# A depthwise-and-projection convolution on one core: an opening that waits for half of image 0, and GpSimd sums that alternate between two tiles

## The reference

```python
v = groupnorm(x)                   # 32 groups = every channel alone, over 64 x 64
xd = concat(v[:, :, 0::2, 0::2], v[:, :, 0::2, 1::2],
            v[:, :, 1::2, 0::2], v[:, :, 1::2, 1::2])   # 128 channels, 32 x 32
feats = concat(dwconv(xd, w1, 1), dwconv(xd, w3, 3), dwconv(xd, w5, 5))
y = einsum('bchw,oc->bohw', feats, w_proj)              # 384 -> 128 channels
out = x + interleave(y)            # the four quarters of y go back to the 2 x 2 positions
```

## Time and profile before

| | |
|---|---|
| median of 3 runs | 137.13 us (136.56 to 137.18) |
| the profiled execution | 136.35 us, of which the trace spans 134.5 us |
| busy | TensorE 94%, VectorE 90%, GpSimd 87%, ScalarE 82% |
| granted TensorE clock | 0.99 on the mean |

### The profile page before, as it was taken

One profiled execution on the slowest core, in us unless ns is written; L12 is line 12 of the kernel. 1 busy time (PEld: TensorE's weight loads), 2 busy tenths in 40 slices (PEclk: granted clock), 3 DMA queues, 4 the chain that ended last, 5 costly groups with the idle time before them and its releaser, 6 DMA issues.

```text
span 134.5 us, 1577 instructions
## 1 busy us (share of the span) xinstructions
PE 126.2 (94%) x519; PEld 97.2 (72%) x519; DVE 120.6 (90%) x147; ACT 110.5 (82%) x118; POOL 117.5 (87%) x89
## 2 busy tenths in 40 slices
PE   5998999999999999999999999999999999999920
PEld 5866888888886888688886888688867688778700
DVE  6579799998799999999999999999999999999660
ACT  2589989999999999999999999999999999060000
POOL 6261999999999999999999999999999999999930
PEclk9999999999999999999999999999999999999996
DMA  3999999990044008097999879693799478989176
GB/s 71 270 258 199 204 202 203 193 189 5 2 80 80 0 0 163 3 117 110 187 124 90 166 156 112 100 188 72 78 103 185 107 78 78 117 134 202 25 169 138
DMA packets 35847, 16.67 MB, mean 124 GB/s; under 512 B 34048, under 2 KB 34176, under 8 KB 35456
## 3 DMA queue, kind: packets, MB, share of 16 engines
q0 software_dynamic: 1488, 6.93, 38.6%
q1 hardware_dynamic: 32720, 9.18, 36.2%
q10 hardware_dynamic: 1632, 0.48, 2.0%
HBM read 5.46 MB, written 4.19 MB: 72 GB/s over the span
## 4 chain that ended last, share of the span: by engine, by line
PE 88%; DMA 4%; ACT 2%; ACTq 1%; DVEq 1%; DVE 1%; issue 0%
PE YP L700 77%; PE YP L763 10%; DMA w_sb<-in_L_conv_w_dram 4%; ACT weff L401 2%; ACT HI L411 1%; DVEq L102 1%; DVE X L657 1%; ACTq L377 0%; ACTq L376 0%; PE YP L675 0%; PE YP L688 0%; ACT coef L395 0%; PE YP L682 0%; ACT coef L406 0%; ACTq L397 0%
## 5 line engine op out<-in xcount | busy, mean ns | idle before, releaser
L324 POOL TENSOR_TENSOR RING_SUM<-RING_SUM,PROD 128x900 f32<-128x900 f32 (+1 forms) x45 | 92.8, 2066 | 3.5
L621 DVE SCALAR_TENSOR_TENSOR ACC<-G,coef,ACC 128x930 f32<-128x930 f32 (+1 forms) x57 | 68.2, 1196 | 1.8
L461 ACT ACTIVATE PROD<-G,coef 128x900 f32<-128x900 f32 (+1 forms) x45 | 44.5, 1050 | 0.0
L700 PE MATMUL YP<-HI,wlo 128*128 128x512 f32 (+2 forms) x148 | 38.8, 412 | 0.0
L700 PE MATMUL YP<-HI,whi 128*128 128x512 f32 (+2 forms) x148 | 36.6, 398 | 0.7 <-ACT HI L411 0.7
L700 PE MATMUL YP<-LO,whi 128*128 128x512 f32 (+2 forms) x148 | 37.2, 401 | 0.0
L700 PEld LDWEIGHTS YP<-HI,wlo 128*128 128x128 f32 x148 | 27.9, 189 | 8.7 <-issue 2.9
L700 PEld LDWEIGHTS YP<-HI,whi 128*128 128x128 f32 x148 | 27.7, 189 | 7.8 <-ACT HI L411 1.1
L700 PEld LDWEIGHTS YP<-LO,whi 128*128 128x128 f32 x148 | 27.9, 189 | 7.1 <-issue 1.0
L421 ACT ACTIVATE G<-X,nbias,rstd 64x1024 f32<-64x1024 f32 x16 | 21.1, 1318 | 0.8 <-DVE nbias L533 0.5
L442 ACT ACTIVATE Y<-YP 64x1024 f32<-64x1024 f32 x14 | 15.3, 1095 | 4.4 <-PE YP L763 4.1
(11 more groups left out here) (67 smaller groups left out, 61.8 us busy)
## 6 DMA issues: line engine op xcount, KB each, us to landing
X<-in_x_dram SPq DMA_DIRECT2D x16, 256.0 KB, 5.9
LO<-G POOLq DMA_DIRECT2D x7, 527.5 KB, 5.2
X<-Y POOLq DMA_DIRECT2D x6, 512.0 KB, 7.3
out_dram<-X SPq DMA_DIRECT2D x12, 256.0 KB, 4.5
out_dram<-X SPq DMA_DIRECT2D x6, 128.0 KB, 2.5
XS<-in_x_dram SPq DMA_DIRECT2D x2, 256.0 KB, 4.3
XS<-in_x_dram SPq DMA_DIRECT2D x1, 512.0 KB, 7.3
out_dram<-X ACTq DMA_DIRECT2D x2, 128.0 KB, 2.8
```

Source lines behind the costliest of these rows:

```text
L324: pool.tensor_tensor(dst, dst, prod(b, k), ALU.add).then_inc(prod_added, 1)
L461: act.activation(prod(b, k), g_tap(b, POOL_OF[b][k + 1]), ACT.Copy, scale=of5(POOL_OF[b][k + 1])).then_inc(prod_ready, 1)
L621: dve.scalar_tensor_tensor(part(ACC, tap), g_tap(b, tap), of5(tap), part(ACC, tap), ALU.mult, ALU.add).then_inc(acc_step, 1)
L700: mm = nc.tensor.matmul(dst, w[:, n, :], src, start=start, stop=False, skip_group_check=True)
```

## The change

- **Loading.** The rows 0 to 16 of image 0 are a transfer of their own with a semaphore of their own, ahead of the rest, and the high half of the top rows waits for them alone.
- **Weights.** TensorE transposes with the permuted identity, ScalarE copies one block of three to `wpT`, and VectorE reads the other two in PSUM. ScalarE scales 5 taps in place of 7, GpSimd 4 in place of 2. On GpSimd all of them, and the three `wlo` splits, stand ahead of the spread of image 1's statistics.
- **GpSimd's sums.** The product with index 1 (tap (-2,-1)) becomes a wide one: 30 full rows of 32 columns. GpSimd adds the products of (-2,-2) and (-2,2) to the wide one and the others to `RING_SUM`, in turn, so that an add follows one on the other tile; the wide one is added to `RING_SUM` last. An add waits for the last one on its own tile where it can.
- **Taps.** `POOL_N` is 6,6,6,7,7,7,7,9 in place of 6,6,6,6,6,7,7,9. TensorE has its outer tap in image 6 only. VectorE has 9, 9 taps in images 3 and 4 in place of 9, 10.
- **Places.** `inv_std` number 3 moves behind the add with index 3 of image 0, `combine` number 2 moves two taps ahead.

```diff
-POOL_TAPS = [(2, 0), (-2, -2), (-2, 2), (2, -2), (2, 2), (-2, -1), (2, 1), (-1, -2), (1, 2)]
-POOL_N = [6, 6, 6, 6, 6, 7, 7, 9]
+POOL_TAPS = [(2, 0), (-2, -2), (-2, -1), (2, -2), (-2, 2), (2, 2), (2, 1), (-1, -2), (1, 2)]
+WIDE = 1
+POOL_N = [6, 6, 6, 7, 7, 7, 7, 9]
-EXTRA_IMAGES = (3, 6)
+EXTRA_IMAGES = (6,)
-ACT_SCALED = 7
+ACT_SCALED = 5
-COMBINE_AT = {(0, 8): (1, 1, 2), (1, 3): (2, 2, PAIRS)}
+COMBINE_AT = {(0, 8): (1, 1, 2), (1, 1): (2, 2, PAIRS)}
-INV_STD_AT = {(0, 2): (3, 2, 3), (1, 2): (4, 3, COLS)}
+INV_STD_AT = {(0, 3): (3, 2, 3), (1, 2): (4, 3, COLS)}
+def wide_takes(b):
+    return [k for k in range(N_PROD[b]) if POOL_OF[b][k + 1] in ((-2, -2), (-2, 2))]
+def sum_order(b):
+    plain = [k for k in range(N_PROD[b]) if k != WIDE and k not in wide_takes(b)]
+    order, takes = [], wide_takes(b)
+    while takes or plain:
+        order += takes[:1] + plain[:1]
+        takes, plain = takes[1:], plain[1:]
+    return order + [WIDE]
...
-            load_image(sp, 0, image_loaded[0])
+            load_image(sp, 0, top_loaded, 0, TOP)
+            load_image(sp, 0, image_loaded[0], TOP, PH)
...
-                for k in range(N_PROD[b]):
+                for k, n in enumerate(sum_order(b)):
                     if k == NEXT_IMAGE_AT and b + 1 < B:
                         low_image(b + 1)
-                    pool.wait_ge(prod_ready, products_before(b) + k + 1)
-                    if k > 0:
-                        pool.wait_ge(prod_added, products_before(b) + k)
-                    dst = part(RING_SUM[:, b % SUMS, :, :], POOL_OF[b][k + 1])
-                    pool.tensor_tensor(dst, dst, prod(b, k), ALU.add).then_inc(prod_added, 1)
+                    (r0, r1), (c0, c1) = prod_area(b, n)
+                    if n in wide_takes(b):
+                        pool.wait_ge(prod_ready, products_before(b) + max(n, WIDE) + 1)
+                        if n != wide_takes(b)[0]:
+                            pool.wait_ge(prod_added, freed_by(b, wide_takes(b)[0]))
+                        dst = prod(b, WIDE)[:, :, c0:c1]
+                    else:
+                        pool.wait_ge(prod_ready, products_before(b) + n + 1)
+                        if k > 1:
+                            pool.wait_ge(prod_added, products_before(b) + (k - 1 if k < 4 else k))
+                        dst = RING_SUM[:, b % SUMS, r0:r1, c0:c1]
+                    pool.tensor_tensor(dst, dst, prod(b, n), ALU.add).then_inc(prod_added, 1)
...
-            for k in (2, 1, 0):
-                copy_wpT(k)
+            act.activation(wpT[:, :], WT_PS[:, 2 * P:3 * P], ACT.Copy).then_inc(wpT_ready, 1)
...
-            act.wait_ge(image_loaded[0], 32)
+            act.wait_ge(top_loaded, 32)
             act.wait_ge(stats_ready, 1)
             high_half(0, TOP, 0, hi_top)
+            act.wait_ge(coef_ready, 2)
+            act.activation(coef[:, W1_AT:N_COEF], COEF_PS[:, W1_AT:N_COEF], ACT.Copy).then_inc(coef_copied, 1)
+            act.wait_ge(image_loaded[0], 32)
             high_half(TOP, PH, 0, hi_bottom)
```

More of the change, by code:

```diff
@@ L46 @@
 N_PROD = [len(taps) - 1 for taps in POOL_OF]
-PROD_SIZE = max((PH - abs(dy)) * (PW - abs(dx)) for taps in POOL_OF for dy, dx in taps[1:])
+PROD_SIZE = (PH - 2) * PW
 LATE = tuple(range(8))
@@ L67, with freed_by, slot_free @@
 RING_AFTER_HIGH = {2: 0, 3: 1, 4: 2, 5: 3, 6: 4, 7: 6}
-COMBINE_AT = {(0, 8): (1, 1, 2), (1, 3): (2, 2, PAIRS)}
+COMBINE_AT = {(0, 8): (1, 1, 2), (1, 1): (2, 2, PAIRS)}
 RING_AFTER_WLO = {6: 5}
 NEXT_IMAGE_AT = 3
-INV_STD_AT = {(0, 2): (3, 2, 3), (1, 2): (4, 3, COLS)}
+INV_STD_AT = {(0, 3): (3, 2, 3), (1, 2): (4, 3, COLS)}
 def products_before(b):
     return sum(N_PROD[:b])
+def wide_takes(b):
[7 more added lines that the diff above has]
+    return order + [WIDE]
+def freed_by(b, k):
+    return products_before(b) + sum_order(b).index(k) + 1
+def slot_free(q):
+    return max(freed_by(b, k) for b in range(B) for k in range(N_PROD[b]) if products_before(b) + k <= q)
 def steps_before(b):
@@ L200, in g_tap, with prod_source @@
             return image(G, b, (2 + dy + r0) * PITCH + PAD + dx + c0, r1 - r0)[:, :, 0:c1 - c0]
+        def prod_source(b, k):
+            dy, dx = POOL_OF[b][k + 1]
+            (r0, r1), (c0, c1) = prod_area(b, k)
+            return image(G, b, (2 + dy + r0) * PITCH + PAD + dx + c0, r1 - r0)[:, :, 0:c1 - c0]
         def part(tile, tap):
@@ L204, in part, with prod_area @@
             return tile[:, r0:r1, c0:c1]
+        def prod_area(b, k):
+            dy, dx = POOL_OF[b][k + 1]
+            return span(dy, 0, PH), (0, PW) if k == WIDE else span(dx, 0, PW)
         def prod(b, k):
-            (r0, r1), (c0, c1) = span(POOL_OF[b][k + 1][0], 0, PH), span(POOL_OF[b][k + 1][1], 0, PW)
+            (r0, r1), (c0, c1) = prod_area(b, k)
             return PROD[:, (products_before(b) + k) % PRODS, 0:(r1 - r0) * (c1 - c0)].rearrange("p (r c) -> p r c", c=c1 - c0)
@@ L316, in sum_products @@
                 pool.wait_ge(first_prod, b + 1)
[L317 removed]
+                rows, cols = prod_area(b, WIDE)
+                for k, n in enumerate(sum_order(b)):
                     if k == NEXT_IMAGE_AT and b + 1 < B:
                         low_image(b + 1)
[L320 to L324 removed]
+                    (r0, r1), (c0, c1) = prod_area(b, n)
[10 more added lines that the diff above has]
+                    pool.tensor_tensor(dst, dst, prod(b, n), ALU.add).then_inc(prod_added, 1)
                     if (b, k) in ADD_X_AT:
@@ L346, in _ @@
             pool.tensor_copy(whi[:, 0:CHUNK, :], weff[:, 0:CHUNK, :]).then_inc(whi0_ready, 1)
-            scale_w5(ACT_SCALED + 1)
-            pool.wait_ge(whi0_ready, 1)
-            pool.wait_ge(whi_ready, CHUNKS - 1)
+            pool.wait_ge(wpT_ready, 1)
+            pool.wait_ge(coef_copied, 1)
+            for n in range(ACT_SCALED, N_INNER):
+                scale_w5(n)
             for k in range(CHUNKS):
                 taps = slice(k * CHUNK, (k + 1) * CHUNK)
+                if k == 0:
+                    pool.wait_ge(whi0_ready, 1)
+                else:
+                    pool.wait_ge(whi_ready, k)
                 pool.tensor_tensor(wlo[:, taps, :], weff[:, taps, :],
                                    whi[:, taps, :].bitcast(F32), ALU.subtract).then_inc(wlo_ready, 1)
[L354 to L357, removed]
+            pool.wait_ge(part_stats, 5)
+            pool.tensor_tensor(spread[:, 1, :, :], stp[:, 1, None, :].to_broadcast([P, PARTS, STATS]),
+                               mask[:, :, None].to_broadcast([P, PARTS, STATS]), ALU.mult).then_inc(spread_done, 1)
             low_image(0)
@@ L557, in bias, with transposed @@
                                       ALU.mult, ALU.mult).then_inc(stats_ready, 1)
+            def transposed(k):
+                return WT_PS[:, k * P:(k + 1) * P]
             def add_w3(*taps):
@@ L580, in _ @@
             part_variance(0)
-            dve.wait_ge(wpT_ready, 2)
+            dve.wait_ge(wt_ready, 1)
             dve.wait_ge(coef_copied, 1)
@@ L762, in ring @@
                     cols = slice(bank * 512, (bank + 1) * 512)
-                    mm = nc.tensor.matmul(YP[:, b % AREAS, cols], wpT[:, 2, :], F[:, b % 2, cols],
+                    mm = nc.tensor.matmul(YP[:, b % AREAS, cols], wpT[:, :], F[:, b % 2, cols],
                                           start=False, stop=True, skip_group_check=True)
```

40 lines of the change are left out of this document (16 added, 24 removed).

## The result

The changed kernel takes 142.43 us, the median of 4 runs (141.96 to 142.6), against 136.88 for the kernel before (its three runs and one more). The ratio is 1.0409, with a 95% interval of 1.0362 to 1.0456, so it is slower by 4%. The prediction was 142.0, in a range of 138.7 to 143.9. The profiled execution took 141.96 us, with a span of 140.2.

The account below looks back on a forecast made before the run. Three engines were taken as balanced to about 1 us. GpSimd's terms, -2.2 + 4.3 + 1.9 - 1.0 + 2.6 = +5.6 us, on the profiled 136.35 gave 141.95 (142.7 by the median); forecast 142.0, range 138.7 to 143.9.

Parts of the forecast that it names:

- The bound: At the end of the kernel, GpSimd's last add of products was to come 5.6 us later, at 130.0, delaying the end.
- Start and pause: Image 0 on GpSimd: first add at 17.8, 1.0 us earlier, then 2.6 us standing before the third add for ScalarE's product.
- Two more products: GpSimd's adds in images 3 and 4: one more product each, with a wait each, +4.3 us.
- Alternation and wide add: GpSimd's adds in all images: twelve waits spared for -2.2 us, eight unbroken wide adds at 2.25 us for +1.9.
- The opening: TensorE's start: fewer ScalarE scalings and an earlier high half save 0.3 us, between 0 and 0.5.
- my lower bound: TensorE's saving in the opening is 0 if VectorE sets the pace.
- Waits behind it: Opening: the late inverse deviation makes VectorE stand about 2 us and TensorE 1.0 us; at the end this is cover.
- Rival 1: TensorE's clock falls before its last matmuls, which take 5.2 us in place of 2.58: 143.4 us at most, chance 0.17.
- the 5.4 us that I took from there to the end: From GpSimd's last adds of image 6, through SyncE's queued stores of image 7, to the span's end: 5.4 us.
- the faster case: GpSimd absorbs everything because adds on alternating tiles run into each other: 135.5 us, chance 0.09.
- the cheap wide add: GpSimd's wide adds cost as the form in rows, 2.6 us less: 139.4; smaller delays to 140.6 together have chance 0.21.

Follow-up runs that it names:

- e3: The changed kernel with ScalarE making the fourth product of image 0 ahead of its work for image 1: 141.1 us, ratio 1.0314 to the kernel before.
- e7: The kernel before with the new distribution of taps alone: 139.66 us, ratio 1.0205 to the kernel before.
- e4: The changed kernel with RING_SUM at a row pitch of 33 elements in place of 32: 141.08 us, ratio 1.0325 to the kernel before.
- e2: The changed kernel with GpSimd's sums as before, all into RING_SUM in product order, no wide product: 139.47 us, ratio 1.0176 to the kernel before.
- e12: As e9, with five idle matmuls ahead of image 0 in place of eight: 136.58 us, ratio 0.9997 to the kernel before.
- e9: The kernel before with the change's opening alone (loading, weights, their order); taps, sums and inv_std 3's place as before: 137.16 us, ratio 1.003.
- e1: The changed kernel with the old distribution of taps; opening and alternating sums stay: 139.07 us, ratio 1.018 to the kernel before.
- e8: The changed kernel with 20 idle matmuls keeping TensorE busy ahead of its last projection: 141.32 us, ratio 1.0348 to the kernel before.
- e10: The changed kernel with taps 6,6,6,6,7,7,7,9, alternation from image 2 on, RING_SUM at row pitch 33, inv_std 3 at its old place: 138.63 us, ratio 1.0147.
- e5: The changed kernel with RING_SUM and all products at a row pitch of 33: 142.35 us, ratio 1.0433 to the kernel before.

## Why the prediction was right, point by point

- **The bound.** GpSimd's sum became the end of the chain, 5.28 us later than before where I had 5.6. The start and the pause give 1.60 of it (1.6), the sums themselves 3.68 (4.0).
- **Start and pause.** First add at 17.95 (17.8), pause 2.51 (2.6). e3 removes the pause, and the adds then end only 0.8 us earlier, since ScalarE's time is missing elsewhere; by the ratios it is 1.3 us, with overlapping intervals.
- **Two more products.** e7 shows 4.2 us in images 3 and 4 (4.3). From the first add to the last it is 109.27 us there and 105.57 before, so 3.7 remain, and by the ratio 2.8 us of time. The term stands, but it was not a plain addend: small waits elsewhere absorb a part.
- **Alternation and wide add.** The wide adds last 2.20 to 2.27 us (2.25) where no lag of a transfer is in them, and e4 confirms 0.2 us each. But over all images the two edits did not win the -2.2 + 1.9 = -0.3. From the first add to the last it is 129.71 - 17.95 - 2.51 = 109.25 us without the pause. With the same taps in the old order it is 127.75 - 18.48 = 109.27 in e7 and 127.26 - 18.21 = 109.05 in e2, so the two edits come to between 0.0 and +0.2. Image 3 shows where a part goes. Two starts lie 1.94 us apart (57.82 to 59.76) where e2 has 2.40, and two others 2.69 apart (62.28 to 64.97) where e2 has 2.40. 0.46 are won behind one transfer and 0.29 given back behind the next; the 0.2 that stay are less than the wide add costs more.
- **The opening.** I took 0.3 us off TensorE, of 0 to 0.5. e12, which has five idle matmuls in place of eight, gives 0.2 in its profile, and neither e9 nor e12 gives anything clear of noise in time. VectorE sets the pace, which was my lower bound: its cast of the second set of weights ends at 11.14 against 11.30, and that of the third at 13.06 against 12.87, after a wait of 0.23 for a weight that GpSimd scales. And the pace of the eight idle matmuls, which I had not looked at, can cost up to 1 us in single executions.
- **Waits behind it.** VectorE waits 1.79 (2), TensorE 0.84 (1.0). Both vanish in the slack at the end, as expected.
- **The fallen clock.** Rival 1 came true in the trace: the clock is at 0.50 from 128.8 on, TensorE having stood idle from 125.96, and the seven last matmuls take 5.0 us in place of 2.57. Its price was mis-sized: 0.8 us, not 1.4, because most of these matmuls lie beside GpSimd's adds of image 6 (to 134.32) and the stores of SyncE's queue. And the 5.4 us that I took from there to the end are 5.1 wherever GpSimd sets the end at full clock (e1, e8, e10); why the kernel before has 0.3 more is not known. So 142.0 held, but partly by errors that cancel: I had the sum 0.3 too high, the stretch behind it 0.3 too long, and in it the clock at nothing in place of 0.8.
- **The other rivals.** GpSimd absorbed nothing, so neither the faster case nor the cheap wide add came.
- **The parts.** The opening alone is +0.4 us (e9, not clear of noise). On top of it the taps are +2.0 (e2 against e9) and the alternation +2.1 (e1 against e9), 4.5 together; the whole is 0.0409 x 136.9 = 5.6. The taps are +2.8 on the kernel before (e7), and undone in the changed kernel the taps give back 3.1 (e1) and the alternation 3.2 (e2). Each ratio has an interval of 0.4 to 1.0 us to either side, so the 1.1 that is missing may be noise in part. The profiles show 0.8 of it: the clock costs that in the changed kernel and nothing in e1, where it stays at 1.00, nor in e2, where its fall is hidden.

## What to carry over

Before an order is changed to spare waits inside one engine, look at when each of its inputs is made: an order that asks for the fourth product third turns slack towards the producer into a pause, and it returns wherever the consumer catches up. The three engines here were balanced to 1 us, so work taken from two of them (1.35 and 1.22 us) could bring nothing, and the third paid 4.2 us of adds for it. A single part's cost is best read from the part undone and the part alone, since waits of tenths elsewhere soak up what a sum over instructions counts.

## What the runs showed of the hardware

- After a transfer that GpSimd issues, its next add shows 2.25 us in place of 2.0. An add that does not wait starts 0.31 us before the end of that one, shows the same length and passes the lag on; a second transfer behind it makes it 2.54. The first add that waits pays it and is back at 2.04. From the changed kernel, image 3:

```profile
57.25 0.81 POOL L380 DMA_DIRECT2D X<-Y  x1
57.82 2.25 POOL L370 TENSOR_TENSOR RING_SUM<-RING_SUM,PROD 128x900 f32<-128x900 f32 x1
59.76 2.23 POOL L370 TENSOR_TENSOR PROD<-PROD 128x900 f32<-128x900 f32 x1
61.66 1.17 POOL L349 DMA_DIRECT2D LO<-G  x1
62.28 2.54 POOL L370 TENSOR_TENSOR RING_SUM<-RING_SUM,PROD 128x900 f32<-128x900 f32 x1
64.97 2.04 POOL L370 TENSOR_TENSOR RING_SUM<-RING_SUM,PROD 128x930 f32<-128x930 f32 x1
```

- GpSimd adds of equal form and size took 1.90 or 2.27 us (e5), it seems by the place of the tiles; the cause is open.
- In the opening TensorE ran the same eight matmuls in 2.06 us in one execution and 3.37 in another.
- Before the last projection TensorE waited 3.01 us in e2 and 2.97 in e10. The clock then fell to 0.50 in e2 and was still at 1.00 through the last matmuls in e10.
